# Moving paddings, sends and three ramp steps between queues in a two-layer gated cross-attention kernel

## The reference

```
x = x + tanh(g_xattn[l]) * cross_attention(layernorm(x), ctx, ctx, mask)
x = x + tanh(g_ffn[l])   * mixture(layernorm(x))
```

## Time and profile before

| | us |
|---|---|
| median of 3 runs | 516.75 |
| runs | 513.42, 516.75, 519.32 |
| the profiled execution, its own time | 511.04 |
| its span, first to last instruction | 509.1 |

### The profile page before, as it was taken

One profiled execution on the slowest core, in us unless ns is written; L12 is line 12 of the kernel. 1 busy time (PEld: TensorE's weight loads), 2 busy tenths in 40 slices (PEclk: granted clock), 3 DMA queues, 4 the chain that ended last, 5 costly groups with the idle time before them and its releaser, 6 DMA issues.

```text
span 509.1 us, 21940 instructions
## 1 busy us (share of the span) xinstructions
PE 439.4 (86%) x8481; PEld 322.0 (63%) x8481; DVE 352.2 (69%) x885; ACT 320.8 (63%) x764; POOL 256.8 (50%) x333
## 2 busy tenths in 40 slices
PE   2698999999988795999997898998998697779996
PEld 1455676767655685999983565666666475445553
DVE  5767879888768765555536778788898587644554
ACT  2456566766856773777745465768777467775653
POOL 2632535647456177445557527454545326634454
PEclk9999999999989998999999899999999999999999
DMA  7125333312001143332114121201041000000112
GB/s 210 52 57 145 91 99 107 103 53 61 25 24 34 40 102 95 87 93 67 39 36 104 24 44 23 45 25 25 13 98 32 14 5 3 2 2 16 42 48 64
DMA packets 39446, 28.60 MB, mean 56 GB/s; under 512 B 12224, under 2 KB 34368, under 8 KB 39344
## 3 DMA queue, kind: packets, MB, share of 16 engines
q1 hardware_dynamic: 29104, 14.61, 11.3%
q0 software_dynamic: 3424, 6.51, 5.1%
q10 hardware_dynamic: 6816, 6.08, 4.2%
HBM read 19.42 MB, written 7.76 MB: 53 GB/s over the span
## 4 chain that ended last, share of the span: by engine, by line
PE 43%; DVE 19%; issue 15%; POOL 11%; ACT 7%; DMA 3%; SPq 0%; POOLq 0%; ACTq 0%; DVEq 0%
PE T_ps L899 8%; DVE maxes L625 7%; POOL y_mid L1173 7%; PE S_ps L888 6%; DVE prob L633 4%; PE A_ps L914 4%; PE m_H_ps L1484 3%; PE S_ps L882 2%; PE Q_ps L869 2%; PE m_X_ps L1511 2%; PE m_T_ps L1524 2%; PE Q_ps L781 2%; PE m_X_ps L1495 2%; POOL sorted_rows L490 2%; PE Q_ps L792 2%
## 5 line engine op out<-in xcount | busy, mean ns | idle before, releaser
L625 DVE TENSOR_REDUCE maxes<-S_ps 128x16 f32<-128x1024 f32 x64 | 78.2, 1221 | 49.4 <-PE S_ps L888 49.4
L441 POOL TENSOR_TENSOR k_blk<-kT,col_a 128x512 f32<-128x512 f32 x64 | 68.4, 1079 | 74.5 <-ACT kT L514 53.8
L556 ACT ACTIVATE probT<-T_ps 128x512 f32<-128x512 f32 x128 | 76.1, 594 | 45.0 <-PE T_ps L899 44.0
L899 PE MATMUL T_ps<-col_a,prob 128*128 128x128 f32 x512 | 84.1, 288 | 15.1 <-DVE prob L633 11.3
L899 PEld LDWEIGHTS T_ps<-col_a,prob 128*128 128x128 f32 x512 | 56.8, 144 | 55.1 <-issue 29.4
L633 DVE TENSOR_TENSOR prob<-S_ps,maxes 128x512 f32<-128x512 f32 x128 | 82.4, 685 | 2.2
L1173 POOL DMA_INDIRECT y_mid<-f_out,f_rows x39 | 37.2, 955 | 31.7 <-DVE f_out L1054 29.3
L914 PE MATMUL A_ps<-v_blk,probT 128*32 128x18 f32 x4096 | 49.0, 187 | 1.6 <-issue 1.6
L914 PEld LDWEIGHTS A_ps<-v_blk,probT 128*32 128x32 f32 x4096 | 42.3, 111 | 11.3 <-issue 10.5
L1043 DVE TENSOR_TENSOR f_hid<-f_H_ps,f_b 128x512 f32<-128x512 f32 x39 | 27.0, 692 | 29.5 <-PE f_H_ps L1225 24.6
L888 PE MATMUL S_ps<-k_blk,qT 32*64 32x256 f32 x1024 | 46.3, 411 | 0.8 <-ACT qT L550 0.3
(11 more groups left out here) (201 smaller groups left out, 873.5 us busy)
## 6 DMA issues: line engine op xcount, KB each, us to landing
f_w<-in_W ACTq DMA_DIRECT2D x16, 256.0 KB, 2.7
ctxT<-in_ctxT SPq DMA_DIRECT2D x12, 256.0 KB, 3.0
f_rows<-sorted_rows SPq DMA_DIRECT2D x39, 64.5 KB, 1.9
out<-m_final SPq DMA_DIRECT2D x32, 64.0 KB, 1.6
x_all<-in_x SPq DMA_DIRECT2D x6, 256.0 KB, 6.2
x_all<-y_mid POOLq DMA_DIRECT2D x6, 256.0 KB, 4.5
ctxT<-in_ctxT SPq DMA_DIRECT2D x8, 128.0 KB, 2.4
mask_in<-in_mask SPq DMA_DIRECT2D x6, 128.0 KB, 3.1
```

The costliest lines, as they stand in the source:

```text
L441: nc.gpsimd.tensor_tensor(k_blk[:, t % 2, :, :, :], kT[:, g.at(R), t - g.first, :].rearrange("p (b k) -> p b k", b=2).unsqueeze(2).to_broa ...
L556: nc.scalar.activation(probT[:, t % 2, 4 * h:4 * h + 4, :], T_ps[:, :, :], ACT.Exp, scale=SCALE).then_inc(probT_ready, 1)
L625: nc.vector.tensor_reduce(maxes[:, t % 2, :, :], S_all[:, :, 0:HQ * S].rearrange("p r (e k) -> p r e k", k=S), X, ALU.max).then_inc(max_re ...
L899: last = nc.tensor.transpose(T_ps[:, j, :], pair, ident[:, :])
```

## The change

Drain: ScalarE pads no longer; SyncE pads experts 0 to 3 and GpSimd 4 to 7, each with a semaphore of its own. GpSimd's list has, at due number 39, the last two scatters, then its paddings, then the sends of tiles 0 to 4; no send is due before 39. `RINGS` goes to 12, `DEEP` to 8, with eight `y_sent` semaphores.

Ramp: the first two `blocks` of layer 1 come before the first two `raise_x`; `norm_shift` of group 13 is due at 31.5, behind the first `maximum` and its two `subtract`; and ScalarE does a one-element Exp (`warm`) in its ramp list, between the second `v_out` and the third `k_out`.

```diff
@@ -455,10 +455,10 @@
         def gpsimd_ahead(pool):
             blocks, raise_x = gpsimd_steps(pool)
+            for t in tiles[:2]:
+                blocks(t)
             for g in groups[BY_SYNC:4]:
                 raise_x(g)
-            for t in tiles[:2]:
-                blocks(t)
...
         def gpsimd(pool):
             def norm(g):
@@ -760,7 +760,7 @@
-            steps = [(norm_shift, groups, head(-9)), (r_norm_shift, groups, settled(4, 7, short, later)), (maximum, tiles, shift(-1)), (subtract(0), tiles, shift(-1)), (subtract(1), tiles, shift(-1)),
+            steps = [(norm_shift, groups, lambda g: g.first - (8.5 if g.i == NG + 3 else 9)), (r_norm_shift, groups, settled(4, 7, short, later)), (maximum, tiles, shift(-1)), (subtract(0), tiles, shift(-1)), (subtract(1), tiles, shift(-1)),
@@ -950,9 +950,10 @@
 def experts0(nc, ctx, space, r, done):
...
-    RINGS = 16
-    DEEP = 4
+    RINGS = 12
+    DEEP = 8
     HIDS = 3
+    PADS_BY_SYNC = 4
...
     def sb(name, shape, dt=F32):
@@ -1001,7 +1002,7 @@
-    ends_padded = sem("ends_padded")
+    ends_padded = {n: sem("ends_padded_" + n) for n in ("sync", "gpsimd")}
@@ -1138,7 +1139,8 @@
             if t == FULL_TILES:
                 sp.wait_ge(table, 2)
                 sp.wait_ge(r["padded"], 16)
-                sp.wait_ge(ends_padded, 16 * E0)
+                sp.wait_ge(ends_padded["sync"], 16 * PADS_BY_SYNC)
+                sp.wait_ge(ends_padded["gpsimd"], 16 * (E0 - PADS_BY_SYNC))
...
             row = sp.value_load(entry(0, t), min_val=0, max_val=ROWS - P)
@@ -1147,17 +1149,17 @@
-    def pad_ends(eng, experts):
+    def pad_ends(eng, experts, padded):
         def step(_):
...
             for e in experts:
                 row = eng.value_load(pad_at[0:1, e:e + 1], min_val=0, max_val=E0 * REGION - P)
-                eng.dma_start(r["sorted"][bass.ds(row, P), :], r["pads"][:, e, :]).then_inc(ends_padded, 16)
+                eng.dma_start(r["sorted"][bass.ds(row, P), :], r["pads"][:, e, :]).then_inc(padded, 16)
...
     def drain_sync(sp):
-        return [(load(sp), range(FULL_TILES), lambda t: FULL_AT + 2.5), (pad_ends(sp, range(0, E0, 2)), once, lambda _: REST_AT)]
+        return [(load(sp), range(FULL_TILES), lambda t: FULL_AT + 2.5), (pad_ends(sp, range(PADS_BY_SYNC), ends_padded["sync"]), once, lambda _: REST_AT)]
...
     def sync(sp):
@@ -1174,6 +1176,11 @@
                                     out[:, t % DEEP, :], None).then_inc(sent[t % DEEP], 16)
...
+    def drain_gpsimd(pool):
+        (send, skew), = tile_gpsimd(pool)
+        return [(pad_ends(pool, range(PADS_BY_SYNC, E0), ends_padded["gpsimd"]), once, lambda _: REST_AT),
+                (send, range(FULL_SLOTS - skew), lambda t: max(slot_at(t + skew), REST_AT))]
+
     def gpsimd(pool):
@@ -1203,7 +1210,7 @@
         sooner, later = tile_scalar(eng)
-        return [(warm, once, lambda _: NT - 0.5)] + placed(sooner, 0.1) + [(pad_ends(eng, range(1, E0, 2)), once, lambda _: REST_AT)] + placed(later)
+        return [(warm, once, lambda _: NT - 0.5)] + placed(sooner, 0.1) + placed(later)
...
     def scalar(eng):
         sooner, later = tile_scalar(eng)
@@ -1257,7 +1264,7 @@
-    return stage, {"sync": drain_sync, "gpsimd": lambda pool: placed(tile_gpsimd(pool)), "scalar": drain_scalar,
+    return stage, {"sync": drain_sync, "gpsimd": drain_gpsimd, "scalar": drain_scalar,
@@ -1598,13 +1605,14 @@
+        warmed = sb("warmed", [P, 1])
...
-                  "y_sent": [sem(f"f0_sent{k}") for k in range(4)],
+                  "y_sent": [sem(f"f0_sent{k}") for k in range(8)],
...
                   "padded": sem("padded"), "casts": sem("casts")}
@@ -1660,6 +1668,9 @@
+        def warm(_):
+            nc.scalar.activation(warmed[:, :], w0["eps"][:, 0:1], ACT.Exp)
+
         def gates(_):
@@ -1801,7 +1812,7 @@
             first.scalar(act)
             experts.scalar(act)
-            run(ahead.scalar(act))
+            run(ahead.scalar(act) + [(warm, once, lambda _: NT + 5.5)])
             then.scalar(act)
...
```

## The result

| | before | after |
|---|---|---|
| median, us | 513.42 (5 runs, 511.59 to 519.32) | 522.18 (5 runs, 518.27 to 525.14) |
| profiled execution, us | 511.04 | 518.27 |
| its span, us | 509.1 | 516.6 |
| mean granted clock | 0.982 | 0.976 |

The ratio is 1.0176, 95% interval 1.0126 to 1.0226: slower by 6.5 to 11.6 us. The profiled execution of after is the fastest of its five, and that of before is faster than all five of before; their spans are 7.5 us apart.

What follows compares the result with a forecast made beforehand. It took TensorE's wait for tile 13 in the drain, then the ramp into layer two, as the bound. Drain +8.7 (+7.0 chain, +1.7 clock) and ramp -2.5 gave +6.2 on the median 516.75: 523.0 us, range 518.0 to 528.0.

Steps and rivals of the forecast that it cites:

- The drain's delay of tile 13: Drain: load(12) waits for send(0), SyncE's paddings and load(13) queue behind; tile 13 turned at 216.4 instead of 209.44, +7.0 us.
- load(13) at 214 or later: Sign that the forecast is right, in SyncE's timeline of the drain: the load of tile 13 comes at 214 or later.
- The other signs: SyncE's 13th load alone near 206, paddings following; TensorE idle before tiles 12 and 13, clock 0.5 after; first maximum right after stats.
- The clock: Drain: TensorE returns from idling at the lower clock and loses 1.7 us after tile 13, 0 if the clock holds.
- TensorE's wait for tile 12: Drain: TensorE idles from 203.2 until load(12) lands at 207.75, 4.5 us.
- The four waits more of DEEP: End of the drain: four more waits on semaphores already high come ahead of the one that counts, 0 us.
- ScalarE's release: Drain: without ScalarE's paddings TensorE finishes slot 11 at about 203.2 instead of 207.5; the 4.3 us are worth nothing without load(12).
- the table load: Ramp, ScalarE: moved ahead it costs 0.2 us on a kT not awaited, at its old place at most 0.3; counted as 0.
- k_blk ahead of the raises: Ramp, GpSimd: two k_blk run in idle time, the first add_y saves 2.17 us, but raised rows are late next; worth nothing.
- The moved shift: Ramp, VectorE: group 13's norm shift after the first maximum, which then follows the stats at 277.05, -2.0 us.
- the one on the other side: Rival, 8%: SyncE issues its paddings before send(0) lands; tile 13 at 208.4, with the ramp -3.5 us, 513.3.
- The longer chain: Rival, 14%: GpSimd's padding pitch is 1.81 us, a padding lands after 3.8; tile 13 at 219.3, in all +9.1 us, 525.9.

Runs made afterwards that it cites:

- the drain alone: The changed kernel with the three ramp steps undone, the drain as changed: 523.09 us, 1.0166 of the kernel before.
- the ramp alone: The kernel before with the three ramp steps of the diff and nothing else: 516.94 us, 1.0006 of the kernel before.

## Why the prediction was right, and where it was not

The direction and the reason held: a new chain begins at send(0), with load(12), the ctx load, SyncE's paddings and load(13) on it, and undoing its cause (one more buffer) takes the whole loss away. The time came out at 522.18 where 523.0 was forecast. That the time lies so close is luck, since it hides two misses. The increase was forecast at 6.2 us and is 8.8 between the medians of five runs; it was added to a median of three, 516.75, that two further runs brought down to 513.42. And the parts were off in both directions.

- *The drain's delay of tile 13*, forecast as +7.0, was over-sized: +3.9 in the profile of after, +5.3 in that of the drain alone. Of the terms, GpSimd's paddings were taken at a pitch of 1.4 us and have 1.03, so from the first of them to send(0) it is 3.93 instead of 5.6 us, near the lower bound; the last scatter ended 2.5 us after the row numbers, as forecast. SyncE's paddings have a pitch of 1.11 instead of 1.22. From the paddings' last issue to load(13), 3.35 us had been summed (2.6 landing and 0.75 address load); 2.54 were measured in after, 3.88 in the drain alone. SyncE waited 1.2 and 2.5 us for the paddings to land there, so the landing makes the difference; why it differs stays open. From the start of send(0) to load(12), 2.35 was forecast and 2.46 measured; load(13) took 1.88 to its turn, forecast 1.9. The profile of after has no landing for SyncE's four paddings; the landing row is that of GpSimd's four:

```profile
DMA to landing us min/median/max: 2.0/2.1/2.3
```

 The median of the earlier trace rows was 2.6, and with one more buffer, where SyncE's paddings run beside them, GpSimd's take 2.8; what makes landings slower wasn't tried. The section that the prediction cites from the Trainium skill, "Anatomy of one DMA" on the page "DMA: Bandwidth & Descriptors", is on DMAs issued by GpSimd, and two of the three links are SyncE's; the sum doesn't rest on it. The sign "load(13) at 214 or later" was not met: it came at 213.19, although the row numbers were 1.7 us later than before. The other signs were.
- *The clock*, forecast as +1.7 behind tile 13: +1.67 in after, +2.5 in the drain alone. But the loss ahead of tile 13, which the step took to go, was still there: after two waits of 0.92 us TensorE ran at 0.50 from 202 to 204. It cost nothing, because TensorE then waits for tile 12. With one more buffer, behind waits of 0.67 and 0.92 us, the clock stayed at 1.00, so what brings it down stays open.
- *TensorE's wait for tile 12* was forecast as 4.5 us and was 2.03: it got through with slot 11 only at 206.42. up(9) started 4.24 us after the row numbers, as forecast (4.3), behind two waits of 0.92 us for VectorE (the pair for the table's list, and bias); what the step lacked is the lower clock behind them, with three times eight matmuls in 1.54, 1.91 and 1.40 us. This changed nothing, because load(13) counts.
- *The four waits more of DEEP, ScalarE's release and the table load* were costed at nothing; no run contradicts that, and for the table load the two times from maximum to exp (2.67 and 2.68) show it.
- *k_blk ahead of the raises* was forecast as worth nothing because the raised rows are late next. They are: add_y fell by 2.15 us and the stat on the raised rows came 9.37 us after the last send's start, before 8.96. With k_blk back, no change in the time can be told. The two k_blk didn't run ahead of the landing, as the step had it, but behind the last send's issue (272.20 to 274.26); that wasn't foreseen, and cost the raises only 0.1 us.
- *The moved shift*, forecast as −2.0, is the step that failed. The first maximum did come 2.24 us earlier. But "the shift itself then stands at 279.7" was costed at nothing, on the ground that ScalarE needs it late. What counts is that VectorE's queue stands behind it: 3.89 us, and the second maximum comes no earlier than before. The earlier trace rows had the warning: a shift of 0.68 us, and an add_y of 2.58. The shift of another group with as many tiles, in the same trace, takes 0.15:

```profile
293.56 0.15 DVE L672 SCALAR_TENSOR_TENSOR shift_by<-stats,rstd 128x4 f32<-128x4 f32 x1
```

 I used the second row for k_blk and not for the instruction that I moved. Put one step later, the shift alone gives about what was forecast: the second maximum 16.58 us after the last send's start with both other steps undone, before 18.60, so −2.0; with all three steps 16.05, so −2.55 against the −2.5 of the whole ramp. From the stat on the raised rows it is 7.27 and 6.97 instead of 9.64, so −2.4 and −2.7.

So the drain cost 1 to 3 us less than forecast, and the ramp gave some 2.5 us less; in the sum the two nearly cancel. The 8.8 us between the medians lie just above the forecast's own spread of +4.5 to +8.5, and the interval, 6.5 to 11.6, reaches into it.

Of the rivals, the one on the other side (SyncE's paddings don't stand behind send(0)) isn't what the change does. In the kernel with load(12) behind the paddings tile 13 was to come 1.0 us earlier than before by this rival, and came 0.9 earlier, but by another path: TensorE didn't wait for tile 13 there, and turned it behind its work on slot 12, so this doesn't test the rival's sum. The longer chain fell, with its pitch of 1.81; the 3.88 us of the drain alone from the last padding to load(13) lie between the forecast's 3.35 and that rival's 4.55.

Thirteen buffers and the later shift are faster than both kernels, than the one before by 0.6 to 1.9% in the version with the fewest other edits. It keeps the paddings on SyncE and GpSimd, the sends behind them, thirteen and seven buffers and the shift at 32.1. It was not run beside the changed kernel itself, so that comparison goes by the kernel before. Why executions of kernels that are the same up to there differ by up to 5 us ahead of the drain (row numbers at 194.94 before, at 200.02 in the ramp alone) stays open.

## What to carry to other kernels

When a ring gets smaller, count the loads that are issued before the first buffer can come free, and read what stands behind the first load that waits: here one missing buffer cost some 2 us itself and the rest through the four paddings in the same queue. When a small VectorE instruction is moved, look at what GpSimd does at its new place as well as at who needs its result: a row that lasts several times as long as the same shape does elsewhere can be a wait that the profile counts as busy. And an absolute time can be met by misses that cancel, so compare the terms, stretch by stretch.

## What the runs showed of the hardware

- A VectorE instruction of four elements for each partition is held for 3.89 us beside four GpSimd instructions in a row, and the profile shows that as busy time; a tensor_reduce (0.15) and a memset (0.06) at the same place aren't. Whether the GpSimd DMA at the head of the train holds it already, or only the k_blk behind, wasn't told apart.
- Four padding DMAs from GpSimd, each with an address that is read at run time, took 0.54 to 0.60 us of the engine each, at pitches of 0.80, 1.15 and 1.14; SyncE's took 0.34 in the median, at a pitch of 1.11. GpSimd sat idle 0.58 and 0.61 us ahead of the third and fourth; that the address load is what it waited for there is read from the order of its queue and wasn't tried.
